# The output projection in fp16 pairs, with Wo and attn scaled

## The chip, the cores and the metric

The kernel runs on one core of one Trainium2 chip. The metric is the device time of one execution in microseconds (us). The time before is 435.67, the median of 3 runs (434.54 to 435.75).

## The reference

One cross-attention layer, with all inputs and outputs in fp32. x is 2 x 2048 x 640, the context 2 x 77 x 1024, with 20 heads of 32. The image part (ip) is empty, since the context has just the 77 text rows.

```
q = split_heads(x @ Wq.T);  k = split_heads(ctx @ Wk.T);  v = split_heads(ctx @ Wv.T)
probs = softmax(q @ k.T / sqrt(32))
out = merge_heads(probs @ v) @ Wo.T + bo + x
```

## The kernel before

Everything is held transposed: channels on the 128 partitions, tokens along the free dimension. The 4096 tokens make NB = 8 tiles of TB = 512 tokens; 640 channels make G = 5 groups of 128 channels, each with HG = 4 heads.

To keep the precision of fp32 at TensorE's fast rates, each large product is made of two parts per operand. An operand a is split into a_hi, a rounded to the narrower kind of number, and a_lo = a - a_hi. `project` (L668) then makes three matmuls per chunk of 128 input channels: w_hi with a_hi, w_lo with a_hi, and w_hi with a_lo. Queries (ps_q) and outputs (ps_o) use pairs of fp32r; probabilities and values use pairs of fp16, where v was divided by the largest value of its channel (v_scale, L515 to L526), which `normalise` (L562) multiplies back in.

The work is a software pipeline, written out by hand per engine. A step (t, g) is one head group g of one token tile t. In step (t, g) the kernel makes the scores and exponentials of (t, g), the max scores of the next group, the query projection of the group after that, the values and the normalisation of the previous group, and one output tile of the previous token tile (`out_tiles`, L63). Every engine runs the same sequence of steps in its own fixed program order (`run`, L118), and semaphores carry the dependencies. Order on TensorE in a steady step (L850 to L889): values of the last group (four column tiles of 32 at once), scores 0 and 1, max scores 0 and 1, output chunks 0 and 1, max scores 2 and 3, scores 2, output chunks 2 and 3, scores 3, transpose of the maxima, output chunk 4, then the whole query projection of 15 matmuls. Steps up to (1, 0) are the fill (L796): the value projections take the place of the outputs. The last token tile's outputs are made at the end, chunk by chunk, in five banks (`last_tiles`, L770).

- ACT: x_hi (L385), k_diag, wq_hi and wo_hi (`w_high`, L400), q_hi (L414), attn_hi (L421), two exponentials per score tile, p_f in fp32 and p_hi in fp16 (L428, L432), and the copy of the transposed maxima (L439). It also issues the loads of the residual x_res and the stores.
- POOL: x_lo (L325), p_lo (L334), attn_lo (L340), wq_lo, wo_lo (L355).
- DVE: the maxima (L548), v_scale, q_lo (L541), the inverse of the denominator and `normalise` (L552 to L566), `finish_out` (L574), which adds bias and residual to ps_o.
- SP: loads of x and the weights, and the DMAs that pack q_hi, q_lo and the maxima into q_packed (`pack_q`, L288; `load_max`, L283).

## Time and profile before

| | |
|---|---|
| median of 3 runs | 435.67 us |
| the profiled execution | 436.16 us, its span 434.4 us |
| mean granted TensorE clock | 0.995 |
| PE busy (matmul) | 426.1 us, 98% of the span, 2538 instructions |
| PE weight load | 313.9 us, 72% |
| POOL | 300.5 us, 69% |
| ACT | 253.9 us, 58% |
| DVE | 232.7 us, 54% |
| share of PE in the chain that ended last | 94% |

The profile is of one execution. Its span runs from the first to the last instruction; the execution's own time also holds what lies around it. PE's busy time counts a matmul from start to modelled end, and matmuls overlap. A row of the order of time that ends in xN merges N instructions. The fp32r matmuls appear as f32 in the rows.

### The profile page before, as it was taken

Reading aid. Unit: us, or ns where it says so; the run is one execution under the profiler, and the core shown is the slowest. Engines: PE = TensorE matmul, PEld = TensorE weight load, DVE = VectorE, ACT = ScalarE, POOL = GpSimd, SP = SyncE. Lnnn points to the kernel's source line nnn. Section 1 sums busy time; section 2 is a strip of 40 time slices with the busy share of each in tenths; the row PEclk is TensorE's granted clock in tenths of the full one; section 3 lists DMA queues with packets and bytes.
Section 4 is the critical chain, followed back from the end, with each engine's and each line's share of the span. In section 5 each row is a group of like instructions: output and inputs, shape, how many; then the busy total and the mean of one; then the engine's idle time right before and its main releaser. Section 6 shows DMA issues by size and latency. Waiting matters only on the chain.

```text
span 434.4 us, 8258 instructions
## 1 busy us (share of the span) xinstructions
PE 426.1 (98%) x2538; PEld 313.9 (72%) x2538; DVE 232.7 (54%) x437; ACT 253.9 (58%) x509; POOL 300.5 (69%) x256
## 2 busy tenths in 40 slices
PE   8999999899999999999999999999999999999996
PEld 6977765677777777777777677777777677777675
DVE  0354766455545555555544555555554455555553
ACT  1737987657465755748464755757564755754510
POOL 8427799989568765959658674959658674955540
PEclk9999999899999999999999999999999999999999
DMA  8997545443455345543355335543355334444203
GB/s 288 359 351 230 203 135 196 146 146 127 145 191 174 122 151 205 205 146 123 135 186 190 123 130 206 204 166 123 125 195 189 124 121 150 157 157 146 75 24 121
DMA packets 39614, 72.68 MB, mean 167 GB/s; under 512 B 5024, under 2 KB 6176, under 8 KB 39584
## 3 DMA queue, kind: packets, MB, share of 16 engines
q1 hardware_dynamic: 28784, 52.62, 34.2%
q10 hardware_dynamic: 10800, 19.67, 14.0%
q8 instruction: 18, 0.29, 0.3%
q14 instruction: 12, 0.10, 0.1%
HBM read 28.81 MB, written 10.49 MB: 90 GB/s over the span
## 4 chain that ended last, share of the span: by engine, by line
PE 94%; POOL 2%; ACT 1%; DVE 1%; issue 1%; DMA 0%; POOLq 0%; ACTq 0%
PE ps_q L673 30%; PE ps_o L673 27%; PE ps_s L731 10%; PE ps_pv L738 7%; PE ps_m L717 5%; PE ps_den L743 4%; PE ps_o L656 2%; POOL p_lo L334 1%; PE ps_m L784 1%; PE ps_s L643 1%; PE ps_m L722 1%; PE ps_q L784 1%; PE ps_q L635 1%; DVE x_f L578 1%; PE ps_o L784 1%
## 5 line engine op out<-in xcount | busy, mean ns | idle before, releaser
L334 POOL TENSOR_TENSOR p_lo<-p_f,p_hi 77x512 f16<-77x512 f32 x160 | 183.2, 1166 | 99.8 <-ACT p_hi L432 97.8
L428 ACT ACTIVATE p_f<-ps_s 77x512 f32<-77x512 f32 x160 | 94.7, 592 | 47.6 <-PE ps_s L731 47.6
L548 DVE TENSOR_REDUCE mx<-ps_m 128x4 f32<-128x308 f32 x160 | 69.3, 475 | 57.7 <-PE ps_m L717 57.4
L432 ACT ACTIVATE p_hi<-ps_s 77x512 f16<-77x512 f32 x160 | 93.5, 584 | 3.0 <-PE ps_den L743 3.0
L541 DVE TENSOR_TENSOR q_lo<-ps_q,q_hi 128x512 fp32r<-128x512 f32 x40 | 27.7, 692 | 101.8 <-ACT q_hi L414 101.8
L673 PE MATMUL ps_q<-x_hi,wq_hi 128*128 128x512 f32 x200 | 79.4, 397 | 0.2 <-POOL wq_lo L348 0.2
L673 PE MATMUL ps_q<-x_lo,wq_hi 128*128 128x512 f32 x200 | 78.3, 391 | 0.0
L673 PE MATMUL ps_q<-x_hi,wq_lo 128*128 128x512 f32 x200 | 78.2, 391 | 0.0
L673 PE MATMUL ps_o<-attn_hi,wo_hi 128*128 128x512 f32 x170 | 70.0, 411 | 0.0
L673 PE MATMUL ps_o<-attn_hi,wo_lo 128*128 128x512 f32 x170 | 67.4, 397 | 0.0
L673 PE MATMUL ps_o<-attn_lo,wo_hi 128*128 128x512 f32 x170 | 67.4, 396 | 0.0
L414 ACT CAST q_hi<-ps_q 128x512 fp32r<-128x512 f32 x40 | 23.4, 584 | 72.3 <-PE ps_q L673 72.0
L731 PE MATMUL ps_s<-q_packed,k_packed 128*77 128x512 f32 x160 | 58.7, 410 | 0.3
L325 POOL TENSOR_TENSOR x_lo<-x_f,x_hi 128x512 fp32r<-128x512 f32 x38 | 48.1, 1300 | 5.9 <-ACT x_hi L385 5.8
L340 POOL TENSOR_TENSOR attn_lo<-attn,attn_hi 128x512 fp32r<-128x512 f32 x38 | 48.5, 1299 | 4.3 <-ACT attn_hi L421 4.3
L673 PEld LDWEIGHTS ps_q<-x_hi,wq_hi 128*128 128x128 f32 x200 | 37.6, 188 | 10.1 <-issue 1.9
L673 PEld LDWEIGHTS ps_q<-x_lo,wq_hi 128*128 128x128 f32 x200 | 37.6, 188 | 8.1
L673 PEld LDWEIGHTS ps_q<-x_hi,wq_lo 128*128 128x128 f32 x200 | 37.6, 188 | 7.7
L673 PEld LDWEIGHTS ps_o<-attn_hi,wo_hi 128*128 128x128 f32 x170 | 32.3, 190 | 7.9
L673 PEld LDWEIGHTS ps_o<-attn_lo,wo_hi 128*128 128x128 f32 x170 | 32.2, 189 | 7.2
L717 PE MATMUL ps_m<-k_diag,q_hi 128*128 128x308 f32 x160 | 37.2, 313 | 0.0
L717 PEld LDWEIGHTS ps_m<-k_diag,q_hi 128*128 128x128 f32 x160 | 30.0, 190 | 9.2 <-issue 0.8
(105 smaller groups left out, 522.1 us busy)
## 6 DMA issues: line engine op xcount, KB each, us to landing
q_packed<-q_hi SPq DMA_DIRECT2D x80, 256.0 KB, 2.5
x_f<-in_x SPq DMA_DIRECT2D x40, 256.0 KB, 3.3
q_packed<-q_lo SPq DMA_DIRECT2D x40, 256.0 KB, 3.2
x_res<-in_x ACTq DMA_DIRECT2D x35, 256.0 KB, 2.7
out<-out_sb ACTq DMA_DIRECT2D x35, 256.0 KB, 2.6
wk_sb<-in_wk SPq DMA_DIRECT2D x8, 320.0 KB, 5.4
wv_sb<-in_wv SPq DMA_DIRECT2D x5, 512.0 KB, 5.9
wq_sb<-in_wq SPq DMA_DIRECT2D x5, 320.0 KB, 5.6
```

Source lines behind the costliest of these rows:

```text
L325: nc.gpsimd.tensor_tensor(x_lo[:, c, :], x_f[:, c, :], x_hi[:, c, :].bitcast(F32), ALU.subtract).then_inc(xlo_pool, 1)
L334: nc.gpsimd.tensor_tensor(p_lo[:, i, :], p_f[:, i, :], p_hi[:, i, :], ALU.subtract).then_inc(plo_done, 1)
L340: nc.gpsimd.tensor_tensor(attn_lo[:, c, :], attn[:, c, :], attn_hi[:, c, :].bitcast(F32), ALU.subtract).then_inc(alo_pool, 1)
L414: nc.scalar.copy(q_hi[:, g % RS, :], ps_q[:, :]).then_inc(qhi_done, 1)
L428: nc.scalar.activation(p_f[:, i, :], ps_s[i % 2][0:L, :], ACT.Exp, scale=SCALE).then_inc(pf_done, 1)
L432: nc.scalar.activation(p_hi[:, i, :], ps_s[i % 2][0:L, :], ACT.Exp, scale=SCALE).then_inc(phi_done, 1)
L541: nc.vector.tensor_tensor(q_lo[:, g % RS, :], ps_q[:, :], q_hi[:, g % RS, :].bitcast(F32), ALU.subtract).then_inc(qlo_done, 1)
L548: nc.vector.tensor_reduce(mx[:, g % RS, :, tt], ps_m[tt % 2][:, 0:HG * L].rearrange("p (h k) -> p h k", k=L), AX_X, ALU.max).then_inc(max_ ...
L673: last = nc.tensor.matmul(ps[:, :], w[:, k, P * c:P * (c + 1)], a[:, c, :], start=(c == 0 and n == 0), stop=(c == G - 1 and n == 2))
L717: nc.tensor.matmul(ps_m[tt % 2][:, 0:HG * L], q_hi[:, g % RS, P * tt:P * (tt + 1)], k_diag[:, g, b, :], start=True, stop=True).then_inc(ms ...
L731: nc.tensor.matmul(ps_s[i % 2][0:L, :], k_packed[:, i, g, L * b:L * (b + 1)], q_packed[:, g % RS, i, :], start=True, stop=True).then_inc(s ...
L738: nc.tensor.matmul(ps_pv[D * i:D * (i + 1), :], v[:, b, P * g + D * i:P * g + D * (i + 1)], p[:, i, :], tile_position=(0, D * i), **flags)
```

## The change

The output projection goes from pairs of fp32r to pairs of fp16. fp16 has a narrow range, so both operands are scaled to the upper part of it, by numbers that the kernel finds itself:

- Wo, per group k of output channels: the largest magnitude in each partition of Wo's group (`wo_largest`, in DVE's steps (0, 1) and (0, 2)) goes into `tops`; a matmul with a matrix of ones (`sum_wo`, in PE's step (0, 3)) sums these over the partitions; the group is multiplied in place by 2^15 over that sum (`wo_scale`).
- attn: the largest v_scale of each partition is summed over partitions in the same way (`sum_v`, in PE's step (0, 4)). `normalise` multiplies by v_rel = v_scale x 2^15 / sum in place of v_scale. The first four groups of token tile 0 come before that number is known: they are normalised without a scale, and `rescale` multiplies them afterwards.
- The product of both scales is taken back in `finish_out` by out_scale in the instruction that added the bias. The bias is added by ACT instead, to the residual (`add_bias`), or to x_f for the last token tile (`add_last_bias`), between the first and the second pair of exponentials of each step.
- Wo's loads stand in SP's steps (-1, 4) and (0, 0), behind pack_q; they stood in steps (0, 0) to (0, 3), before pack_q. wo_hi is made in the same steps as wo_lo; wo_lo's steps are changed as shown. wo_sb no longer shares its place with wo_lo.

The diff, cut to its core:

```diff
+    def wo_top_at(t, g):
+
+        return {(0, 1): ((0,), (1,)), (0, 2): ((2,), (3, 4))}.get((t, g), ((), ())) if isinstance(t, int) else ((), ())
+
+    def wo_scale_at(t, g):
+
+        return {(0, 3): (0, 1), (1, 0): (2, 3), (1, 1): (4,)}.get((t, g), ()) if isinstance(t, int) else ()
...
-        return {(0, 3): (0,), (0, 4): (1, 2), (1, 1): (3, 4)}.get((t, g), ()) if isinstance(t, int) else ()
+        return {(0, 4): (0,), (1, 1): (1, 2, 3), (1, 3): (4,)}.get((t, g), ()) if isinstance(t, int) else ()
...
-        wo_hi = sb("wo_hi", [P, G, C], F32R)
-        with ExitStack() as start_up:
-            wo_sb = sb("wo_sb", [P, G, C], F32, start_up)
-        wo_lo = sb("wo_lo", [P, G, C], F32R)
+        wo_sb = sb("wo_sb", [P, G, C], F32)
+        wo_hi = sb("wo_hi", [P, G, C], F16)
+        wo_lo = sb("wo_lo", [P, G, C], F16)
...
-        attn_hi = sb("attn_hi", [P, G, TB], F32R)
-        attn_lo = sb("attn_lo", [P, G, TB], F32R)
+        attn_hi = sb("attn_hi", [P, G, TB], F16)
+        attn_lo = sb("attn_lo", [P, G, TB], F16)
...
+                if exists(shift(t, g, 2)[0]):
+                    pack_q(*shift(t, g, 2))
                 for c in wo_chunks(t, g):
                     sp.dma_start(wo_sb[:, c, :], wo[:, c, :]).then_inc(wo_in[c], 16)
-                if exists(shift(t, g, 2)[0]):
-                    pack_q(*shift(t, g, 2))
...
+            def add_bias(t, k):
+                act.wait_ge(res_in[k % RS], 16 * slot_uses(t, k))
+                nc.scalar.add(x_res[:, k % RS, :], x_res[:, k % RS, :], bias[:, k:k + 1]).then_inc(res_done, 1)
+
+            def add_last_bias(k):
+                act.wait_ge(xlo_pool, G * NB - len(FIRST_DVE))
+                nc.scalar.add(x_f[:, k, :], x_f[:, k, :], bias[:, k:k + 1]).then_inc(last_biased, 1)
...
                     exponentials(t, g, 0)
+                for tile in out_tiles(t, g):
+                    add_bias(*tile)
+                if is_last(t):
+                    add_last_bias(g)
+                if exists(t):
                     exponentials(t, g, 1)
...
+            def wo_largest(groups):
+                for k in groups:
+                    dve.wait_ge(wo_in[k], 16)
+                    nc.vector.tensor_reduce(tops[:, k:k + 1], wo_sb[:, k, :], AX_X, ALU.max,
+                                            apply_absolute_value=True).then_inc(tops_done, 1)
+
+            def v_largest():
+                dve.wait_ge(vscale_done, 3 * G)
+                nc.vector.tensor_reduce(tops[:, G:G + 1], v_scale[:, :], AX_X, ALU.max).then_inc(tops_done, 1)
+
+            def find_wo_scales():
+
+                dve.wait_ge(wo_summed, 1)
+                nc.vector.tensor_scalar(sums[:, 0:G], ps_wsum, TINY, None, ALU.max).then_inc(scale_done, 1)
+                dve.wait_ge(scale_done, 1)
+                nc.vector.reciprocal(ups[:, 0:G], sums[:, 0:G]).then_inc(scale_done, 1)
+
+            def find_v_scale():
+
+                dve.wait_ge(v_summed, 1)
+                nc.vector.tensor_scalar(sums[:, G:G + 1], ps_vsum, TINY, None, ALU.max).then_inc(scale_done, 1)
+                dve.wait_ge(scale_done, 3)
+                nc.vector.reciprocal(ups[:, G:G + 1], sums[:, G:G + 1]).then_inc(scale_done, 1)
+                nc.vector.tensor_scalar(out_scale[:, :], sums[:, 0:G], sums[:, G:G + 1], 1.0 / (UP * UP),
+                                        ALU.mult, ALU.mult).then_inc(scale_done, 1)
+                dve.wait_ge(scale_done, 4)
+                nc.vector.tensor_scalar(v_rel[:, :], v_scale[:, :], ups[:, G:G + 1], UP,
+                                        ALU.mult, ALU.mult).then_inc(scale_done, 1)
+                dve.wait_ge(scale_done, 6)
+
+            def wo_scale(groups):
+                if groups:
+                    dve.wait_ge(scale_done, 2)
+                for k in groups:
+                    nc.vector.tensor_scalar(wo_sb[:, k, :], wo_sb[:, k, :], ups[:, k:k + 1], UP,
+                                            ALU.mult, ALU.mult).then_inc(wo_scaled, 1)
+
+            def rescale(g):
+
+                dve.wait_ge(norm_done, g + 1)
+                nc.vector.tensor_scalar(attn[:, g, :], attn[:, g, :], v_rel[:, g:g + 1], None,
+                                        ALU.mult).then_inc(rescaled, 1)
...
+                if isinstance(t, int) and t == 0 and g < G - 1:
+                    nc.vector.tensor_tensor(attn[:, g, :], ps_pv[:, :], rden[:, :], ALU.mult).then_inc(norm_done, 1)
+                    return
+                nc.vector.scalar_tensor_tensor(attn[:, g, :], ps_pv[:, :], v_rel[:, g:g + 1], rden[:, :],
...
-                nc.vector.scalar_tensor_tensor(out_sb[:, k % RS, :], out_bank(t, k)[:, :], bias[:, k:k + 1],
-                                               x_res[:, k % RS, :], ALU.add, ALU.add).then_inc(outs_done, 1)
+                nc.vector.scalar_tensor_tensor(out_sb[:, k % RS, :], out_bank(t, k)[:, :], out_scale[:, k:k + 1],
+                                               x_res[:, k % RS, :], ALU.mult, ALU.add).then_inc(outs_done, 1)
...
+                if is_scaling(*shift(t, g, -1)):
+                    rescale(2)
+                    rescale(3)
...
                     q_low(*shift(t, g, 2))
+                if is_scaling(t, g):
+                    rescale(0)
+                    rescale(1)
+                wo_scale(wo_scale_at(t, g))
...
+            def sum_wo(t, g):
+
+                pe.wait_ge(max_done, TT * nth(t, g) + 1)
+                pe.wait_ge(ones_done, 1)
+                pe.wait_ge(tops_done, G)
+                nc.tensor.matmul(ps_wsum, all_ones[:, :], tops[:, 0:G], start=True, stop=True).then_inc(wo_summed, 1)
+
+            def sum_v():
+
+                pe.wait_ge(tops_done, G + 1)
+                pe.wait_ge(vlo_done, G)
+                nc.tensor.matmul(ps_vsum, all_ones[:, :], tops[:, G:G + 1], start=True,
+                                 stop=True).then_inc(v_summed, 1)
```

## Rows read from the trace of the kernel before

**Rows 1.** The page: busy us, share of the span, instructions; then the chain by line.
```profile
PE 426.1 (98%) x2538; PEld 313.9 (72%) x2538; DVE 232.7 (54%) x437; ACT 253.9 (58%) x509; POOL 300.5 (69%) x256
...
PE ps_q L673 30%; PE ps_o L673 27%; PE ps_s L731 10%; PE ps_pv L738 7%; PE ps_m L717 5%; PE ps_den L743 4%; PE ps_o L656 2%; POOL p_lo L334 1%; PE ps_m L784 1%; PE ps_s L643 1%; PE ps_m L722 1%; PE ps_q L784 1%; PE ps_q L635 1%; DVE x_f L578 1%; PE ps_o L784 1%
```
**Rows 2.** Waits of PE: who waited for whom, us in total, times, longest.
```profile
PE ps_pv L738 <- POOL p_lo L334: 1.9, 2, 1.5
```
**Rows 3.** PE in order of time, one steady step: start, duration, what, [idle before].
```profile
211.23 0.39 PE L673 MATMUL ps_o<-attn_hi,wo_hi 128*128 128x512 f32 x1
...
212.39 0.40 PE L673 MATMUL ps_o<-attn_lo,wo_hi 128*128 128x512 f32 x1
...
215.55 0.40 PE L673 MATMUL ps_q<-x_hi,wq_hi 128*128 128x512 f32 x1
...
218.73 0.39 PE L673 MATMUL ps_q<-x_lo,wq_hi 128*128 128x512 f32 x1
219.05 0.40 PE L738 MATMUL ps_pv<-p_hi,v_hi 77*32 77x512 f16 x4
...
219.92 0.39 PE L743 MATMUL ps_den<-p_lo,ones 77*32 77x512 f16 x4
```
**Rows 4.** Stretches: length, then busy PE, PEld, DVE, ACT, POOL, PE clock, DMA, GB/s.
```profile
81.50:84.90 3.40, 3.40 (x11) 2.72 (x10) 0.87 (x2) 2.04 (x4) 3.40 (x4) 0.50 0.57 206
...
170.10:219.20 49.10, 49.10 (x299) 36.01 (x295) 27.10 (x50) 30.12 (x60) 35.25 (x30) 1.00 0.46 161
```
**Rows 5.** PE in order of time: first and last of 45 matmuls at the end.
```profile
420.61 0.39 PE L784 MATMUL ps_q<-attn_hi,wo_hi 128*128 128x512 f32 x1
...
430.58 0.39 PE L784 MATMUL ps_s<-attn_lo,wo_hi 128*128 128x512 f32 x1
```
**Rows 6.** Groups: xcount, busy us, mean ns of one, idle before and what ended it.
```profile
L673 PE MATMUL ps_o<-attn_hi,wo_hi 128*128 128x512 f32 x170 | 70.0, 411 | 0.0
...
L385 ACT CAST x_hi<-x_f 128x512 fp32r<-128x512 f32 x40 | 24.5, 620 | 2.8 <-PE ps_q L673 1.5
...
L521 DVE TENSOR_SCALAR v_scale<-v_scale 128x1 f32<-128x1 f32 x5 | 0.8, 153 | 0.2
```
**Rows 7.** Weight loads in order of time, in the warm-up at the start.
```profile
3.15 0.15 PEld L635 LDWEIGHTS ps_q<-v_hi 77*128 77x128 f16 x1 [0.28 <-issue]
...
4.00 0.15 PEld L635 LDWEIGHTS ps_q<-v_hi 77*128 77x128 f16 x1 [0.28 <-issue]
```
**Rows 8.** ACT, POOL and PE in order of time, step (4, 0) and the next.
```profile
229.08 0.58 ACT L414 CAST q_hi<-ps_q 128x512 fp32r<-128x512 f32 x1 [1.33 <-PE ps_q L673]
...
225.49 2.29 POOL L334 TENSOR_TENSOR p_lo<-p_f,p_hi 77x512 f16<-77x512 f32 x2
...
229.55 0.39 PE L738 MATMUL ps_pv<-p_lo,v_hi 77*32 77x512 f16 x4
```
**Rows 9.** DMA issues: engine, op, xcount, KB each, median us to landing.
```profile
wo_sb<-in_wo SPq DMA_DIRECT2D x5, 320.0 KB, 3.3
```
**Rows 10.** POOL, PE, ACT, DVE in order of time, around steps (1, 0) and (1, 1).
```profile
71.68 3.08 POOL L355 TENSOR_TENSOR wo_lo<-wo_sb,wo_hi 128x640 fp32r<-128x640 f32 x2
...
80.56 0.40 PE L738 MATMUL ps_pv<-p_lo,v_hi 77*32 77x512 f16 x4 [1.47 <-POOL p_lo L334]
...
77.90 1.64 ACT L421 CAST attn_hi<-attn 128x512 fp32r<-128x512 f32 x3
79.44 0.57 ACT L414 CAST q_hi<-ps_q 128x512 fp32r<-128x512 f32 x1
...
77.21 0.75 DVE L566 SCALAR_TENSOR_TENSOR attn<-ps_pv,v_scale,rden 128x512 f32<-128x512 f32 x1
...
82.24 0.87 DVE L548 TENSOR_REDUCE mx<-ps_m 128x4 f32<-128x308 f32 x2 [1.50 <-PE ps_m L717]
```
**Rows 11.** Two lines of DVE: xcount, ns min/median/max, first and last start, forms.
```profile
L571 DVE TENSOR_TENSOR attn_lo<-attn,attn_hi x2: 1774/2228/2682, 412.3 to 414.9; 128x512 fp32r<-128x512 f32 x2
...
L536 DVE TENSOR_TENSOR x_lo<-x_f,x_hi x2: 685/952/1219, 14.9 to 16.1; 128x512 fp32r<-128x512 f32 x2
```

More of the change, by code:

```diff
@@ L37, in xattn_kernel @@
     TINY = 1e-30
+    UP = 2.0 ** 15
     WARM_UP = 8
@@ L212, in xattn_kernel @@
         ps_v, ps_vt = ps_o[:, 0:BL], ps_o[0:L, 512 - B * P:512]
+        ps_wsum, ps_vsum = ps_m[0][:, HG * L:HG * L + G], ps_o[:, 0:1]
         ps_last = [ps_q, ps_m[0], ps_m[1], ps_o, ps_s[0]]
@@ L339, in attn_low @@
                     pool.wait_ge(ahi_done, G * t + c + 1)
-                    nc.gpsimd.tensor_tensor(attn_lo[:, c, :], attn[:, c, :], attn_hi[:, c, :].bitcast(F32),
+                    nc.gpsimd.tensor_tensor(attn_lo[:, c, :], attn[:, c, :], attn_hi[:, c, :],
                                             ALU.subtract).then_inc(alo_pool, 1)
@@ L418, in attn_high @@
                     act.wait_ge(norm_done, G * t + c + 1)
+                    if isinstance(t, int) and t == 0 and c < G - 1:
+                        act.wait_ge(rescaled, c + 1)
                     if exists(t - 1):
@@ L570, in attn_low @@
                 dve.wait_ge(ahi_done, G * t + c + 1)
-                nc.vector.tensor_tensor(attn_lo[:, c, :], attn[:, c, :], attn_hi[:, c, :].bitcast(F32),
+                nc.vector.tensor_tensor(attn_lo[:, c, :], attn[:, c, :], attn_hi[:, c, :],
                                         ALU.subtract).then_inc(alo_dve, 1)
@@ L767, in project_out @@
                     pe.wait_ge(outs_done, nth(t, k))
+                elif chunks[0] == 0:
+                    pe.wait_ge(scale_done, 3)
                 project(out_bank(t, k), wo_hi, wo_lo, attn_hi, attn_lo, k, chunks, ready, o_chunks)
```

47 lines of the change are left out of this document (38 added, 9 removed).

## The prediction

> **What bounds the kernel now.** I read the page's busy times and its chain, then TensorE's waits, then its order of time. PE is busy for 98% of the span, and the largest part of the chain that ended last is PE's query projection [rows 1]. In the whole span PE waits 1.9 us for another engine, in two waits, the longest 1.5 us [rows 2]. So an edit changes the time only if it changes the pace at which PE starts matmuls, or opens a wait. Busy time says nothing of the pace, since a matmul lasts 0.39 us and the next starts before it ends; the reader has to subtract starts. In one steady step the six ps_o matmuls from 211.23 to 212.39 are 1.16 / 5 = 0.232 us apart, the fifteen fp32r matmuls of ps_q from 215.55 to 218.73 are 3.18 / 14 = 0.227 apart, and the five fp16 groups of the values from 219.05 to 219.92 are 0.87 / 4 = 0.2175 apart, though all stream 512 columns [rows 3]. The granted clock is 1.00 there, the 2.4 GHz level [rows 4], at which 512 columns take 0.2133 us. fp16 runs near that floor, fp32r 0.014 to 0.019 above it. At the end, where hardly anything else runs, 45 matmuls start in 9.97 us, 0.2266 apart [rows 5]: that excess comes with fp32r, and up to 0.005 more while other engines work. The change can win only this small excess, many times.
>
> **The PE stream.** No matmul is removed. ps_o has 170 triples [rows 6] and the one tile that is made in ps_q five more: 525 matmuls between other work. last_tiles has 5 x 5 x 3 = 75. The nearest row to a 128x128 fp16 weight load with 512 columns at the higher clock is the values' 0.2175, with loads of 32 columns and three extra starts in each group of four. Below stands the floor, 0.2133; above, nothing changes, 0.232. I take 0.216. The warm-up does load 128 fp16 columns, but its starts, 3.15 to 4.00 over two, are 0.425 apart [rows 7], which is 512 columns at 1.2 GHz: any excess that small is hidden at the lower level. Interleaved: 525 x (0.232 - 0.216) = 8.4 us. The end: 75 x (0.2266 - 0.216) = 0.8 us. Together -9.2 us (the floor would give -10.8, the values' own pace -8.3).
>
> PE loses time where it goes from the whole array to the values' four column tiles: 218.73 to 219.05 is 0.32, some 0.10 over the pace [rows 3]. After the change TensorE alternates between fp16 and fp32r six times a step (into and out of ps_o at the max scores, the scores and the transposed maxima), always on the whole array. Below 0; above 0.10 each, since that boundary is one of number kind as well as of tiles. I take 0, because the tiles are reason enough for it; the other reading is the first rival. The Trainium skill, TensorEngine Tiling (Array Packing), section Key Properties, says that changing the tiling mode drains TensorE, and names no drain for a change of number kind. By that rule the alternations are free and the sum stands.
>
> Two matmuls are added, ones times tops, of 5 and of 1 columns: below 0, above a 512-column one each, 0.46 together. I take +0.3.
>
> **ACT.** Each step with an output tile gains one pass over 128x512 between the first and second pair of exponentials; x_hi, of that shape, takes 0.62 [rows 6]. ACT was busy 30.12 of 49.1 us over five steps [rows 4]. Behind the pass stand the exponentials, copy_max, and in step 0 of a tile the attn_hi casts. That is the tightest step: ACT still idled 1.33 before q_hi at 229.08, and the last p_lo ended at 227.78 for a matmul that started at 229.55, 1.77 of slack [rows 8]. 0.6 fits into both, also with a step 15 x 0.016 = 0.24 shorter. The residual it waits for was ordered one step earlier. Cost 0; without that cover up to 0.6 in each of some 35 steps, 21 us, which the slack excludes. finish_out keeps its form with one add made a multiply: 0. Wo's five casts move later and were hidden: 0.
>
> **SP.** Wo's five loads go into two early steps, behind pack_q instead of before it; one lands in 3.3 us [rows 9]. The packed queries come up to 1 us earlier, the next transposed maxima queue behind Wo's loads. From -1 to +3.3; I take 0, since the maxima are ordered some us after those loads.
>
> **DVE and POOL, once, in the fill.** DVE gains five reductions over Wo, seven tiny instructions (v_scale's take 0.153 each, [rows 6]), a reduction over v_scale, five scalings of Wo and four rescalings of attn. Most stand where DVE waits for PE; 0 for these, up to 1 if the two scale computations hold the maxima. The narrow place is 77 to 86 us. There the values waited 1.47 for p_lo until 80.56, since POOL had two wo_lo, 3.08 us, ahead of that step's p_lo [rows 10]. One of them moves to step (1,1): from -1.5 to 0; I take -0.7, since the exponentials are late next. But behind the normalise that ends at 77.96 come two rescalings, and attn_hi of chunks 2 to 4, which began at 77.90, now waits for them; q_hi (79.44) is behind these on ACT, the max scores wait for q_hi on PE, and the scalings of Wo's chunks 2 and 3 stand before the max reductions that began at 82.24 [rows 10], for which PE waits too. No row has a scaling in SBUF. The nearest is a DVE subtraction of 128x512: 0.685 at its fastest, 1.774 and 2.682 while POOL works beside it [rows 11]; POOL is busy here. Below 0.3 (half the fastest), above 2.7 each. At 0.7 each PE hardly notices; at 2.2 the first two hold q_hi to about 83.5, 2 us late, and the scalings add up to 2. I take +1.2 in all. The low clock after the wait (0.50 for 3.4 us, [rows 4]) costs 1.7; I leave it standing. Net here +0.5, between -3.2 (no wait, no low clock) and +4.
>
> In this the trace agrees in kind with the Trainium skill, SBUF — State Buffer, section Who interferes with whom, on the port pair that VectorE and GpSimd share: one instruction of VectorE or GpSimd holds it whole, and a tensor_scalar between SBUF tiles can need it, so a rescaling would wait out one POOL instruction. By it each costs under 2 us, and the net would be +0.5 to +1.
>
> **Sum** against the profiled execution (436.16, its span 434.4): -9.2 + 0.3 + 0.5 = -8.4, so 427.8. The median of the runs, 435.67, is 0.5 lower: **427.3**. With every term at its low end 436.2 - 10.8 - 3.2 = 422.2, or 421.7 by the median; at its high end 436.2 - 8.3 + 0.5 + 4 = 432.4, or 431.9.
>
> **Rivals.** First, slower: each alternation of fp16 and fp32r drains PE as the tiles' boundary does. Place: six per step in 35 steps, 210 in all. Price: 0.10 each, 21 us, so 427.3 + 21 = 448. It turns the result at 8.4 / 210 = 0.04 us each. For it: every boundary of fp16 and fp32r in the steady trace carries 0.1. Against it: all of these are tile boundaries too. Chance 0.11.
>
> Second, no gain: the 0.014 belongs to loading 128 columns of weights, and the values are fast since they load 32. Then the stream stays, and 435.7 + 0.8 = 436.5. For it: no row separates the two. Against it: the weight load of ps_o lasts less than a start-to-start interval in a pace of 0.227 and lies beside a matmul. Chance 0.08.
>
> Third, the stream wins, but the place at 77 to 86 us costs its +4: 427.3 + 3.5 = 430.8. For it: the two slow subtractions beside POOL; against it, POOL waits in that step for ACT, and leaves DVE room. Chance 0.10. The forecast keeps 0.71.
>
> The range 423.5 to 434 holds the forecast and the third rival and leaves out the others, 0.19. A measurement here can tell 0.3% from no change, 1.3 us. Faster: 0.71 + 0.10 = 0.81; the same: 0.08; slower: 0.11.
>
> **What would show it.** ps_o starts about 0.216 apart, and the last 45 in 9.5 us; five steady steps in about 47.9 and not 49.1, with no wait of PE in them; max scores to ps_o and back without a new gap; each rescaling's duration, and what PE waits for between 77 and 86 us. A pace of 0.227 or more in ps_o, or 0.3 between an fp16 and an fp32r matmul on the whole array, makes the forecast wrong.

## The result: 0.6% slower, and the profile after

The changed kernel takes 437.97 us (median of 20 runs, 435.35 to 444.96), the kernel before 435.69 (20 runs, 434.3 to 436.7): ratio 1.0057, 95% interval 1.0037 to 1.0078. The forecast was 427.3 us. Ratios here and below are of fast runs alone, and so leave out 444.96 and one run of the experiment wo768, 845.39. The profiled execution took 438.97, its span 437.2.

The page after, busy times and chain, against [rows 1]:
```profile
PE 423.4 (97%) x2542; PEld 259.5 (59%) x2542; DVE 247.2 (57%) x458; ACT 275.0 (63%) x549; POOL 296.1 (68%) x257
...
PE ps_q L791 29%; PE ps_o L791 25%; PE ps_s L849 9%; PE ps_pv L856 7%; PE ps_m L835 5%; PE ps_den L861 4%; DMA q_packed<-mxT 3%; PE ps_o L760 1%; DVE attn L611 1%; PE ps_m L904 1%; PE ps_s L747 1%; PE ps_m L840 1%; PE ps_q L739 1%; PE ps_q L904 1%; ACT p_hi L461 1%
```
TensorE's waits after, against [rows 2]: who waited for whom, us in total, times, longest.
```profile
PE ps_m L835 <- ACT q_hi L441: 3.1, 1, 3.1
PE ps_s L849 <- DMA q_packed<-mxT: 1.8, 2, 0.9
...
PE ps_m L835 <- DVE mx L634: 1.1, 1, 1.1
PE ps_s L849 <- ACT p_hi L461: 0.6, 2, 0.3
```
PE's busy time fell by 2.7 us, as an fp16 matmul starts sooner. But VectorE's `attn L611`, one of the new rescalings, is in the chain, and these four kinds of wait are new, 6.6 us together. The 1.9 us for p_lo are gone.

The PE stream after in order of time, against [rows 3]: query matmuls, then output matmuls, then the change from fp16 to fp32r (in the last three lines).
```profile
211.08 0.39 PE L791 MATMUL ps_q<-x_hi,wq_hi 128*128 128x512 f32 x1
...
213.66 0.40 PE L791 MATMUL ps_q<-x_lo,wq_hi 128*128 128x512 f32 x1
...
217.81 0.39 PE L791 MATMUL ps_o<-attn_hi,wo_hi 128*128 128x512 f16 x1
...
218.90 0.38 PE L791 MATMUL ps_o<-attn_lo,wo_hi 128*128 128x512 f16 x1
...
219.89 0.38 PE L791 MATMUL ps_o<-attn_lo,wo_hi 128*128 128x512 f16 x1
219.92 0.58 PE L791 MATMUL ps_q<-x_hi,wq_hi 128*128 128x512 f32 x1
220.34 0.39 PE L791 MATMUL ps_q<-x_hi,wq_lo 128*128 128x512 f32 x1
```
The output matmuls are 1.09 / 5 = 0.218 apart by these rounded starts, 0.216 over all steps. At a change of type the next start is shown after 0.03 and the one behind it after 0.42, together 0.45 for two matmuls, which at their own paces would take 0.216 + 0.234: little is lost. What nobody touched got slower: the query matmuls are (213.66 - 211.08) / 11 = 0.2345 apart, where they were 0.227.

At the end, against [rows 5]: 44 intervals in 9.50 us, 0.216.
```profile
423.58 0.38 PE L904 MATMUL ps_s<-attn_lo,wo_hi 128*128 128x512 f16 x1
...
433.08 0.38 PE L904 MATMUL ps_s<-attn_hi,wo_lo 128*128 128x512 f16 x1
```
VectorE, POOL (GpSimd) and ScalarE after in the narrow place, against [rows 10]: start, duration, line, what. An x2 row holds two instructions.
```profile
72.43 2.22 DVE L594 TENSOR_SCALAR out_scale<-sums 128x5 f32<-128x5 f32 x1
...
75.42 1.78 DVE L611 TENSOR_SCALAR attn<-attn,v_rel 128x512 f32<-128x512 f32 x2
77.12 1.84 DVE L634 TENSOR_REDUCE mx<-ps_m 128x4 f32<-128x308 f32 x4
...
81.32 3.64 DVE L611 TENSOR_SCALAR attn<-attn,v_rel 128x512 f32<-128x512 f32 x2
86.69 0.69 DVE L627 TENSOR_TENSOR q_lo<-ps_q,q_hi 128x512 fp32r<-128x512 f32 x1 [1.74 <-ACT q_hi L441]
87.30 2.42 DVE L605 TENSOR_SCALAR wo_sb<-wo_sb,ups 128x640 f32<-128x640 f32 x2
...
73.22 1.40 POOL L377 TENSOR_TENSOR wo_lo<-wo_sb,wo_hi 128x640 f16<-128x640 f32 x1
...
82.17 2.50 POOL L362 TENSOR_TENSOR attn_lo<-attn,attn_hi 128x512 f16<-128x512 f32 x2
...
85.04 0.62 ACT L450 CAST attn_hi<-attn 128x512 f16<-128x512 f32 x1 [1.79 <-DVE attn L611]
...
86.09 0.57 ACT L441 CAST q_hi<-ps_q 128x512 fp32r<-128x512 f32 x1
```
Five elements a partition take VectorE 2.22 us: `out_scale` ends at 74.65, POOL's `wo_lo` at 74.62. The second pair of rescalings ends at 84.96, 0.29 after POOL's two `attn_lo`. The maxima begin late behind the first pair. Behind the second come ScalarE's copies, behind these q_hi, at 86.09 and not at 79.44, and behind q_hi TensorE's `ps_m`, which waits 3.1 us.

Stretches after, against [rows 4]: 3.4 us at half clock come again, after the wait of 3.1, and 49.1 us of the steady state are as full of PE as before.
```profile
86.70:90.10 3.40, 3.38 (x8) 1.28 (x8) 3.40 (x5) 2.62 (x5) 3.19 (x4) 0.51 0.73 275
170.10:219.20 49.10, 49.10 (x299) 29.68 (x298) 27.53 (x52) 33.04 (x67) 35.05 (x31) 1.00 0.46 162
```
Where the time goes is read best from the first matmul of each group's values, which opens the next step. Below are these starts in order of time; the four right-hand kernels are experiments told of further on (pairs: the fp16 pairs alone; pad: the change with its tensors shifted; Wo: pad without attn's scaling; Wo, ACT: that with Wo's scaling on ScalarE and the last biases spread).
```
values of   before   after   pairs     pad      Wo  Wo,ACT
(0,1)        48.20   49.53   48.10   49.49   48.11   49.05
(0,4)        72.03   73.62   71.95   73.51   71.94   72.89
(1,0)        78.26   81.75   78.19   81.65   78.19   79.12
(1,1)        91.34   96.92   89.04   96.78   91.77   89.58
(1,2)       101.16  107.01   98.72  106.85  101.83   99.86
(7,1)       386.14  388.92  378.65  386.80  381.78  379.80
(7,2)       395.95  398.63  388.29  396.44  391.42  389.43
(7,3)       405.80  408.63  397.74  406.42  401.40  398.89
(7,4)       415.87  419.36  407.40  417.14  412.12  409.00
span         434.4   437.2   425.2   435.0   429.9   426.8
```
From before to after, 5.85 us are lost by (1,2): 1.33 by (0,1), 0.26 more by (0,4), 1.90 in the step to (1,0), which holds out_scale and the first pair of rescalings, and 2.36 from there, with the second pair. The 1.33 don't come in every run: the column Wo has the same loads and maxima of Wo up to there, and 48.11. The 29 steady steps from (1,2) to (7,1) win back only 3.07: each takes 9.721 us in place of 9.827, 0.11 less, where 0.24 was forecast. From (7,1) to (7,4) 0.7 are lost, and the outputs at the end win as much.

### The profile page after: what moved, and what is told of

Read it like the earlier page. It is cut to its first block, busy times and chain, and to the rows that moved or that the text cites. A ratio compares the mean times of both kernels' runs of the same rounds, so it can differ in the third digit from the quotient of the medians.

```text
span 437.2 us, 8356 instructions
## 1 busy us (share of the span) xinstructions
PE 423.4 (97%) x2542; PEld 259.5 (59%) x2542; DVE 247.2 (57%) x458; ACT 275.0 (63%) x549; POOL 296.1 (68%) x257
## 4 chain that ended last, share of the span: by engine, by line
PE 89%; DVE 4%; DMA 3%; ACT 2%; issue 2%; DVEq 0%; ACTq 0%
PE ps_q L791 29%; PE ps_o L791 25%; PE ps_s L849 9%; PE ps_pv L856 7%; PE ps_m L835 5%; PE ps_den L861 4%; DMA q_packed<-mxT 3%; PE ps_o L760 1%; DVE attn L611 1%; PE ps_m L904 1%; PE ps_s L747 1%; PE ps_m L840 1%; PE ps_q L739 1%; PE ps_q L904 1%; ACT p_hi L461 1%
## 5 line engine op out<-in xcount | busy, mean ns | idle before, releaser
L791 PE MATMUL ps_q<-x_hi,wq_hi 128*128 128x512 f32 x200 | 86.7, 433 | 0.5 <-DVE q_lo L627 0.2
L849 PE MATMUL ps_s<-q_packed,k_packed 128*77 128x512 f32 x160 | 65.1, 448 | 2.6 <-DMA q_packed<-mxT 1.8
L791 PE MATMUL ps_o<-attn_hi,wo_hi 128*128 128x512 f16 x170 | 65.6, 386 | 0.0
L791 PE MATMUL ps_o<-attn_lo,wo_hi 128*128 128x512 f16 x170 | 64.9, 382 | 0.0
L791 PE MATMUL ps_o<-attn_hi,wo_lo 128*128 128x512 f16 x170 | 64.9, 382 | 0.0
L835 PE MATMUL ps_m<-k_diag,q_hi 128*128 128x308 f32 x160 | 44.0, 353 | 4.2 <-ACT q_hi L441 3.1
L362 POOL TENSOR_TENSOR attn_lo<-attn,attn_hi 128x512 f16<-128x512 f32 x38 | 44.0, 1180 | 4.8 <-ACT attn_hi L450 4.8
L849 PEld LDWEIGHTS ps_s<-q_packed,k_packed 128*77 128x77 f32 x160 | 20.3, 146 | 24.1 <-issue 14.4
L791 PEld LDWEIGHTS ps_o<-attn_hi,wo_hi 128*128 128x128 f16 x170 | 16.5, 97 | 24.1 <-issue 8.6
```

Source lines behind the costliest of these rows:

```text
L362: nc.gpsimd.tensor_tensor(attn_lo[:, c, :], attn[:, c, :], attn_hi[:, c, :], ALU.subtract).then_inc(alo_pool, 1)
L791: last = nc.tensor.matmul(ps[:, :], w[:, k, P * c:P * (c + 1)], a[:, c, :], start=(c == 0 and n == 0), stop=(c == G - 1 and n == 2))
L835: nc.tensor.matmul(ps_m[tt % 2][:, 0:HG * L], q_hi[:, g % RS, P * tt:P * (tt + 1)], k_diag[:, g, b, :], start=True, stop=True).then_inc(ms ...
L849: nc.tensor.matmul(ps_s[i % 2][0:L, :], k_packed[:, i, g, L * b:L * (b + 1)], q_packed[:, g % RS, i, :], start=True, stop=True).then_inc(s ...
```

## The experiments

Ratios are to the kernel before, on the same chip, with their 95% intervals; 0.001 is 0.44 us. Each trace is of one run. A cut in an edit is marked by ..., and remarks behind # are mine.

**Places of the operands.** The change puts 672 bytes a partition of small tensors ahead of x_hi, x_lo and the packed queries. Three kernels move operands and nothing else:
```diff
         all_ones = sb("all_ones", [P, P], F32)
+        pad = sb("pad", [P, 24], F32)     # place768: 96 bytes; place704: [P, 8], 32 bytes
         k_packed = sb("k_packed", [P, HG, G, BL], F32R)
```
before32 has the pad of 32 bytes ahead of k_packed in the kernel before, behind the weights wo_hi and wo_lo.

> The kernel after, with a pad of 96 bytes a partition behind the six new small tensors, so that they take 768 bytes in place of 672 and x_hi, x_lo, q_hi, q_packed and the rest start at multiples of 128 bytes again, as in the kernel before (in after they start 32 bytes past one). No instruction is changed. Theory A (the places of the operands slow the fp32r matmuls): the 15 query matmuls of a step, 233.8 ns each in after and 227.8 in before, go back to 228; over 35 steps 15 x 0.006 x 35 = 3.1 us, and the maxima with them: 1.0057 - 0.007 = 0.998 to 0.999 of the kernel before, 434.6 to 435.2 us. Rival B (they are slowed by something else in after: the fp16 matmuls before them, other transfers, other traffic of the engines): the pace stays at 233.8 and the ratio at 1.004 to 1.008.

> The same with a pad of 32 bytes: all that stands behind it starts 64 bytes past a multiple of 128, on a multiple of 64. Theory A with a boundary of 64 bytes: query matmuls at 228 ns and 0.998 to 0.999 of the kernel before, as with the pad of 96 bytes. Theory A with a boundary of 128 bytes: 233.8 ns and 1.004 to 1.008. Rival B: no change, 1.004 to 1.008, whatever the pad of 96 bytes shows would have to be the same here.

> The kernel before with one unused tensor of 32 bytes a partition ahead of k_packed, so that all behind it stands 32 bytes further; no instruction is changed and nothing is in fp16 pairs. Theory A: both the query and the output projection read moved activations, so 30 matmuls of a step go from 228 to 234 ns: 30 x 0.006 x 40 = 7.2 us, 441 to 443.5 us, ratio 1.012 to 1.018. Rival B: no change, 435.7 us, ratio within 0.003 of 1.

Measured: place768 1.0023 (1.0000 to 1.0046), place704 1.0058 (1.0030 to 1.0085), before32 1.0103 (1.0079 to 1.0127). Query matmuls in order of time, place768, then before32:
```profile
219.42 0.39 PE L792 MATMUL ps_q<-x_hi,wq_lo 128*128 128x512 f32 x1
...
222.40 0.39 PE L792 MATMUL ps_q<-x_lo,wq_hi 128*128 128x512 f32 x1
```
```profile
215.92 0.40 PE L674 MATMUL ps_q<-x_hi,wq_hi 128*128 128x512 f32 x1
...
219.18 0.39 PE L674 MATMUL ps_q<-x_lo,wq_hi 128*128 128x512 f32 x1
```
2.98 / 13 = 0.229 with x_hi on a multiple of 128 bytes, 3.26 / 14 = 0.233 at 32 past it, with no fp16 weights at all, and 0.233 at 64 past it (place704, whose ratio is as expected, too). By these paces theory A holds, with 128 bytes as the boundary. The steady step of the change goes from 9.721 to 9.653 with the pad of 96 bytes, and to 9.706 with that of 32. By the ratio place768 won about half of what was expected, and its interval overlaps those of place704 and of the change: that it saves time at all rests on the traces. before32 lost less than was expected (4.5 us, not 7.2), since its output matmuls between other work slow by 0.002, not 0.006. At its end, where hardly anything else runs, they slow by 0.007, against [rows 5]:
```profile
423.40 0.39 PE L785 MATMUL ps_q<-attn_hi,wo_hi 128*128 128x512 f32 x1
...
433.67 0.39 PE L785 MATMUL ps_s<-attn_lo,wo_hi 128*128 128x512 f32 x1
```
That is 10.27 / 44 = 0.233 where it was 0.2266. The weights of these matmuls had not moved, only the moving operands, attn's highs and lows. The output matmuls of the change, in fp16 at 0.216, have the same pace with and without the shift: of these two, only fp32r pays.

**The early Wo loads.**
```diff
-        return {-1: (0, 1), 0: (2, 3, 4)}.get(nth(t, g), ()) if isinstance(t, int) else ()
+        return {-1: (0,), 0: (1, 2), 1: (3, 4)}.get(nth(t, g), ()) if isinstance(t, int) else ()
```


> The kernel after with the five Wo loads spread 1, 2, 2 over the steps (-1,4), (0,0) and (0,1) in place of 2, 3 over the first two. The transposed maxima of group 1 landed at 48.87 us in after (issued at 43.82, behind three Wo loads of 640 KB in all) and at 46.70 in before. Theory C (these loads hold up the maxima): they land about 1 us earlier, the wait of 0.92 us of the scores at 48.9 us is down to under 0.3, and the kernel is 0.6 to 1.2 us faster than after: 436.8 to 437.4, ratio 1.003 to 1.004. Rival: the wait is another's or the gain is given back at the next waits of the fill: 1.0045 to 1.007.

Measured: 1.0164 (1.0129 to 1.0198), 4.7 us slower than the change by the ratios. VectorE's waits between 38 and 60 us:
```profile
DVE tops L574 <- DMA wo_sb<-in_wo: 5.0, 2, 4.4
```
The maxima of Wo stayed where they were, so VectorE, in order, stood 4.4 us for its own load. That priced a mistake of the experiment, not the theory, which f_loads below tries again.

**VectorE's scalings: their form, and their engine.** Both on place768. forms768 writes each rescaling as
```diff
-                nc.vector.tensor_scalar(attn[:, g, :], attn[:, g, :], v_rel[:, g:g + 1], None,
-                                        ALU.mult).then_inc(rescaled, 1)
+                nc.vector.scalar_tensor_tensor(
+                    attn[:, g, :].rearrange("p (a b) -> p a b", b=P),
+                    attn[:, g, :].rearrange("p (a b) -> p a b", b=P), v_rel[:, g:g + 1],
+                    all_ones[:, :].unsqueeze(1).to_broadcast([P, TB // P, P]), ALU.mult, ALU.mult).then_inc(rescaled, 1)
```
and Wo's scalings, out_scale and v_rel likewise with two tensors. act768 takes the same scalings out of VectorE's stream and puts them into ScalarE's, for attn
```diff
+                        nc.scalar.mul(attn[:, c, :], attn[:, c, :], v_rel[:, c:c + 1]).then_inc(rescaled, 1)
```
ahead of the wait and the copy in attn_high, and for Wo in the same way in wo_high.

> The kernel after with the pad of 96 bytes, and with another form of VectorE instruction for the scalings that the change added on SBUF operands: the four rescalings of attn, the five of Wo, out_scale and v_rel were tensor_scalar (one tensor read) and are now scalar_tensor_tensor or tensor_tensor (two tensors read; the second is a tensor of ones or the scale itself). The same products on the same engine at the same place of its stream, and the 2^15 is folded into the sums. In after the nine tensor_scalar of 128x512 and 128x640 took 1.2 to 3.6 us each and the one of 128x5 2.22, while POOL's subtractions ran; normalise, a two-tensor form of 128x512, took 0.69 beside the same subtractions. Theory A (a one-tensor SBUF form of VectorE waits for GpSimd's running operation): each rescaling takes 0.7 us, out_scale 0.2; the values of group (0,4) and after, 3.4 us late against before at 81.65 us and 5.7 at 106.85, come about 1.5 and 3 us earlier: 2.0 to 3.5 us under the kernel with the pad alone, ratio 0.994 to 0.998. Rival B (they are long because of what they wait for, or in any form): the rescalings stay over 1.5 us and the ratio at 1.0023.

> The kernel after with the pad of 96 bytes, and with the rescalings of attn and of Wo, v_rel and out_scale moved from VectorE to ScalarE, which does each directly ahead of the copy to fp16 that it does anyway. Theory A (the loss of the fill is VectorE's scalings, each 1.2 to 3.6 us long beside GpSimd): VectorE's maxima and q_lo come early again, ScalarE carries nine passes more of 0.7 us, four of them in the step that starts at 81.65 us, so 1 to 3 us are won and up to 1 lost on ScalarE: ratio 0.995 to 1.001. Rival B (what bounds the narrow place is ScalarE's chain through q_hi, which these passes now lengthen by 2.8 us): the values of step (1,1) come no earlier than 96.8 us and the ratio is 1.002 to 1.009.

Measured: forms768 1.0057 (1.0031 to 1.0083), not faster than place768 (the intervals overlap; in the profiled runs it is 3.1 us later at (1,2)); act768 0.9979 (0.9965 to 0.9993), 1.9 us faster than place768, as its theory A had it. Groups of VectorE between 70 and 95 us, forms768:
```profile
L615 DVE SCALAR_TENSOR_TENSOR attn<-attn,v_rel,all_ones 128x512 f32<-128x512 f32 x4 | 6.4, 1650 | 0.0
...
L596 DVE TENSOR_TENSOR out_scale<-sums 128x5 f32<-128x5 f32 x1 | 2.3, 2260 | 0.0
```
My idea that only the one-tensor form waits was wrong: the two-tensor form waits as well, 1.65 each. (The 3.6 us in the expectation is a row of two instructions: singly the rescalings of the change took 0.48, 1.39, 1.22 and 2.49.) normalise and q_lo, of the same size, take 0.75 and 0.69 in the same stretch: they read one tensor from PSUM and one from SBUF, the scalings read only SBUF. The Trainium skill, SBUF — State Buffer, section Who interferes with whom, has both halves: a tensor_scalar between SBUF tiles can take the pair of ports that VectorE shares with GpSimd, and two inputs in SBUF contend with a GpSimd instruction that reads SBUF. The traces agree with both, by the 1.39 to 2.49 of the one form beside POOL and the 1.65 of the other. They also show more than one instruction waited for: the last rescaling of the change, 2.49 us from 82.46, began while POOL's `attn_lo` of 82.17 to 83.56 ran and ended only after the next one, at 84.95.

**The last biases.**
```diff
-                if is_last(t):
-                    add_last_bias(g)
+                if is_last(t) and g == 0:
+                    add_last_bias(0)
...
+                if is_last(t) and g in (1, 2):      # behind exponential 3
+                    add_last_bias(2 * g - 1)
+                    add_last_bias(2 * g)
```


> The kernel after with the pad of 96 bytes, and with the bias of the last five tiles added at the ends of the steps (7,1) and (7,2), two each, and one in (7,0), in place of one in each of (7,0) to (7,4); (7,3), which has two bias passes of its own, and (7,4) lose one. In after ScalarE's passes there held up the exponentials: waits of 0.31 and 0.26 us of the scores, and 0.6 more ahead of the last tiles; the stretch from the values of (7,3) to the values of the last step took 10.72 us in place of 10.07. Theory: 0.3 to 0.8 us faster than the kernel with the pad alone, ratio 1.0005 to 1.0017, and the stretch is at 10.1 to 10.4. Rival (the stretch is longer by a wait on VectorE or on the alternation): no change, 1.0023 and 10.7.

Measured: 0.9983 (0.9958 to 1.0008). The steps (7,3) and (7,4) take 9.45 and 10.12 us, where place768 has 9.98 and 10.72: 1.1 us. The ratio says 1.7 us, more than was expected, but its interval overlaps that of place768, and the rest lies ahead of the edit, in the fill of the profiled run, so I put 1.1 down to it.

**Price of a change of type.** alt768 is place768, altbefore the kernel before, each with
```diff
-                if tiles:
-                    project_out(*tiles[0], (0, 1))
-                if exists(max_t):
-                    max_scores(max_t, max_g, 2, batch(max_t))
...
+                for c in range(4):
+                    if tiles:
+                        project_out(*tiles[0], (c,))
+                    if exists(max_t) and c < 2:
+                        max_scores(max_t, max_g, 2 + c, batch(max_t))
+                    if exists(t) and c == 2:
+                        scores(t, g, 2, batch(t))
```

> The kernel after with the pad of 96 bytes; in each steady step the fp16 output matmuls are cut finer, by groups of three: three, one fp32r matmul of maxima, three, maxima, three, scores 2, three, where it was six, two of maxima, scores 2, six. That makes 10 changes of type a step in place of 6. Step now 9.65 us. By the 0.05 us a step that six changes seem to cost (7.834 us of the stretch of output, maxima, scores and query matmuls less 0.24 of pace would be 7.594, measured 7.643), four more cost 0.03: 9.68. By the rival of the prediction, 0.10 each, 10.05. Nothing but the order is changed; the same order in the kernel before is the control, to be run after this.

> The control: the kernel before, all fp32r in these matmuls, with the same finer order of output, maxima and score matmuls (three, maxima, three, maxima, three, scores, three). There is no change of type in it. Step now 9.82. If the step of the fp16 kernel with this order (9.733 against 9.65) is longer by the four more changes of type (0.02 each), this one stays at 9.82 within 0.02. If it is by the order itself, 9.90.

Measured, over the 29 steady steps: alt768 9.757 against 9.653, +0.104; altbefore 9.869 against 9.827, +0.042. alt768 is above the 9.68 expected, altbefore between its 9.82 and 9.90: the order itself costs 0.04, and four more changes of type 0.062, 0.015 each, by one profiled run of either kernel. Six of them would be 0.09 a step. The steady step gives less. With the pad it is 0.17 shorter than before; the output matmuls of the kernel before start 0.2305 apart in the mean of all steady steps, not 0.232 as in the step of [rows 3], so the pace wins 15 x 0.0145 = 0.22, and 0.05 are left, 0.008 for each of the six.

**The fp16 pairs alone.** This is the kernel before with Wo's and attn's pairs in fp16, without any scale, with bias and loads as before; wo_sb gets a place of its own, as in the change.
```diff
-        wo_hi = sb("wo_hi", [P, G, C], F32R)
+        wo_hi = sb("wo_hi", [P, G, C], F16)       # wo_lo, attn_hi, attn_lo likewise
```


> The kernel before with one part of the change alone: Wo's and attn's highs and lows are fp16 in place of fp32r. It leaves out all scaling of the change (the maxima and sums of Wo, the rescalings, out_scale) and the moved bias, so the lows of Wo and attn lose low bits. Every tensor behind the Wo ones stands where it stands in the kernel before, on a multiple of 128 bytes. Theory: the steady step is at 9.65 us as in the kernel after with the pad of 96 bytes (9.82 before), which gives 35 x 0.17 = 6.0 us, the end 0.7 more, and the fill loses nothing, since what it lost were the scalings beside GpSimd and the early Wo loads: 428.5 to 430, ratio 0.984 to 0.988. Rival: the fill loses its time by the alternation or by the clock as well, 432 to 434, ratio 0.992 to 0.996.

Measured: 427.01 us, 0.9816 (0.9800 to 0.9833), 8.0 us faster and better than expected; five runs within 0.23 us. The steady step is at 9.653, as with the pad. The granted clock in the stretch of [rows 4]:
```profile
81.50:84.90 3.40, 3.40 (x19) 1.75 (x18) 2.61 (x7) 2.71 (x6) 3.40 (x4) 1.00 0.54 197
```
It holds 2.4 GHz here, after a wait for p_lo of 1.0 us in place of 1.5, and is 2.4 us ahead by (1,2). This was not in the expectation. The kernel before itself does both: of its 90 runs beside the experiments, 51 have a mean clock of 0.998 or more and a median of 434.58 us, 38 have 0.995 or 0.996 and 435.95. So a stretch at half clock costs it 1.4 us, and against its runs without one the pairs win 7.6. None of the 20 runs of the change is above 0.996.

**Repairs together.** best2 is act768 with the spread biases; best3 adds later Wo loads, and the maxima with them.

> The kernel after with three repairs: the pad of 96 bytes, the scalings on ScalarE, and the last biases spread over (7,0) to (7,2). Alone the second gave 0.9979 against 1.0023 with the pad alone (2.0 us), the third 0.9983. If they add up: 1.0023 - 0.0044 - 0.001 to 0.004 = 0.994 to 0.997, 432.6 to 434.0. Rival: they share what they gain, since the spread can only bear on the end of the program (0.6 us there) and the rest of its figure was the spread of runs: 0.9965 to 0.998.

> best2 with the Wo loads spread 1, 2, 2 over (-1,4), (0,0), (0,1), as in the kernel that came out slower for it (there VectorE, in order, waited 4.4 us for the Wo load that its maxima need), and now with the maxima of Wo moved behind the loads: groups 0 | 1 | 2 | 3, 4 at the steps (0,1) to (0,3). Theory C (the early loads cost 1.2 us by holding up the transposed maxima on the way in): no wait of VectorE on Wo, 0.5 to 1.3 us faster than best2, ratio 0.0012 to 0.003 under it. Rival: the two maxima in (0,3), 1.6 us ahead of the sum over the partitions, hold up TensorE there, and it is not faster than best2 (0 to 0.003 above it).

Measured: best2 0.9957 (0.9942 to 0.9972), as expected, best3 0.9941 (0.9920 to 0.9962). best3 has its values of (0,1) at 48.17, not 49.11 as best2 (wo768 has 48.11 there with the loads unchanged, so this can be chance), but its profiled span is 1.1 us longer (432.3 against 431.2), with 6.8 us at half clock in the narrow place where best2 has 3.4. The intervals overlap, so its gain is not settled.

**Each part on the pairs alone.** f_rdve and f_ract multiply the four attn chunks by 1.0 on VectorE or on ScalarE, f_loads has the change's Wo loads, f_bias its bias.
```diff
+                nc.vector.tensor_scalar(attn[:, g, :], attn[:, g, :], 1.0, None, ALU.mult).then_inc(rescaled, 1)  # f_rdve
+                nc.scalar.mul(attn[:, c, :], attn[:, c, :], 1.0).then_inc(rescaled, 1)  # f_ract, ahead of its copy
+                for c in {-1: (0, 1), 0: (2, 3, 4)}.get(nth(t, g), ()) if isinstance(t, int) else ():  # f_loads, behind pack_q
+                nc.scalar.add(x_res[:, k % RS, :], x_res[:, k % RS, :], bias[:, k:k + 1]).then_inc(res_done, 1)  # f_bias
```


> The kernel with the fp16 pairs alone (no scales, bias on VectorE, Wo loads at their old places: 427.0 us, 0.9816) and four in-place multiplications of attn by 1.0 on VectorE (tensor_scalar, 128x512), at the places of the change's rescalings and waited for by ScalarE's copies to fp16. Theory A (they wait for GpSimd's running subtraction, and later ones for two): 0.5 us where GpSimd is idle, 1.2 to 2.5 beside it, q_hi of step (1,0) late, a wait of 2 to 3 us of TensorE and then a stretch at the low clock: 2.5 to 5 us, ratio 0.987 to 0.993. Rival B (they are short and hidden here, and only together with the scale computations and loads do they matter): under 1 us, 0.981 to 0.984.

> The same with the four multiplications on ScalarE, each directly ahead of its copy to fp16. Theory A: ScalarE has no turn to wait for, each takes 0.7 us; 1 to 2.5 us, ratio 0.984 to 0.9875, and in any case less than with VectorE. Rival B (any 2.8 us more ahead of q_hi in step (1,0) costs the same, whoever does it): the same ratio as with VectorE within 0.001.

> The kernel with the fp16 pairs alone, and its five Wo loads at the change's places: two in (-1,4), three in (0,0), behind the queries' packing. Nothing else. Theory C (the early loads delay the maxima and the packed queries on the same queues): the values of (0,1), at 48.10 us there and at 49.53 in after, come 0.8 to 1.3 us later; 0.8 to 1.5 us in all, ratio 0.9834 to 0.985. Rival (that delay was VectorE's maxima of Wo, 0.8 us each ahead of the maxima of the scores): 0 to 0.3 us, 0.981 to 0.9825.

> The kernel with the fp16 pairs alone, and the bias as in the change: ScalarE adds it to the residual ahead of exponential 1 of each step, and to the last five tiles in (7,0) to (7,4). Nothing else. Theory: nothing in the steady steps (9.65 us), and 0.5 to 1.7 us at the end, where (7,3) has three passes; ratio 0.983 to 0.9855. Rival (ScalarE's slack hides it there too): 0.981 to 0.9825.

Measured: f_rdve 0.9900 (0.9867 to 0.9933), f_ract 0.9898 (0.9869 to 0.9926), f_loads 0.9831 (0.9802 to 0.9859), f_bias 0.9850 (0.9819 to 0.9880), so 3.7, 3.6, 0.7 and 1.5 us over the pairs alone (each of these differences is uncertain by some 1.5 us, and the last two intervals overlap that of the pairs). VectorE in f_rdve, and what TensorE waited for:
```profile
71.87 4.60 DVE L573 TENSOR_SCALAR attn<-attn 128x512 f32<-128x512 f32 x2
76.39 0.85 DVE L550 TENSOR_REDUCE mx<-ps_m 128x4 f32<-128x308 f32 x2
...
80.80 0.75 DVE L573 TENSOR_SCALAR attn<-attn 128x512 f32<-128x512 f32 x2
```
```profile
PE ps_m L729 <- DVE mx L550: 3.1, 1, 3.1
```
The first pair takes 4.60 us (2.20 and 2.48) beside POOL's two `wo_lo` and two `p_lo`, the second 0.75 (0.42 each) with POOL idle: the same instruction, six times as long, and it holds the maxima. In f_ract each takes 0.61, but two of them and three copies stand between the last exponential and q_hi, two more before:
```profile
79.09 0.61 ACT L420 ACTIVATE attn<-attn 128x512 f32<-128x512 f32 x1
...
81.96 0.58 ACT L414 CAST q_hi<-ps_q 128x512 fp32r<-128x512 f32 x1
```
and the half clock follows, here two of the stretches of f_ract, columns as in [rows 4]:
```profile
82.00:84.00 2.00, 1.57 (x5) 0.82 (x5) 1.43 (x3) 2.00 (x6) 2.00 (x3) 0.50 0.56 176
84.00:86.00 2.00, 2.00 (x6) 0.95 (x5) 0.12 (x1) 0.48 (x1) 2.00 (x3) 0.50 0.92 333
```
Rival B of f_ract held, the same ratio within 0.001, but the two profiled runs lose in different ways. f_rdve adds the wait of 3.1 us and has 3.4 us at half clock. In f_ract TensorE waits at most 1.1 us at a time, for p_hi, p_lo and q_hi, and the half clock lasts 6.8 us, in which output matmuls start 0.43 apart and not 0.216: it costs 3.4. That the ratios are equal may therefore be chance. The loss is shown for either engine, but not that work ahead of q_hi has one price. As expected, f_bias has its 1.6 us in the steps (7,3) and (7,4), 9.99 and 10.72 where the pairs alone have 9.45 and 9.66; its steady step is unchanged. f_loads lies between theory and rival, its profile shows 0.2, and its 0.7 is not clear of noise.

**The Wo part and the attn part, in the whole change.** wo768 is place768 without attn's scaling: the rescalings, v_rel, the sum over v and the second factor of out_scale are left out. wobest moves Wo's scalings to ScalarE as well, and spreads the last biases.
```diff
-                nc.vector.scalar_tensor_tensor(attn[:, g, :], ps_pv[:, :], v_rel[:, g:g + 1], rden[:, :],
+                nc.vector.scalar_tensor_tensor(attn[:, g, :], ps_pv[:, :], v_scale[:, g:g + 1], rden[:, :],
```


> The kernel after with the pad of 96 bytes, and without the scaling of attn: normalise multiplies by v_scale as before the change, and the sum of v's maxima, v_rel, the four rescalings and the second factor of out_scale are left out; out_scale is the sum of Wo's maxima alone. Wo is still loaded early, reduced, summed and scaled on VectorE, and the bias is still on ScalarE. If the attn part costs here what the rescalings cost alone (3.7 us), plus the out_scale that took 2.2 us of VectorE: 4 to 6 us under the kernel with the pad alone, ratio 0.988 to 0.993. If most of the 5 us that are left are Wo's: no more than 3.7 us under it, ratio 0.994 to 0.997.

> The same with Wo's five scalings moved to ScalarE, ahead of its copies, and the last biases spread over (7,0) to (7,2), which won 1.1 us of the 1.6 at the end in two kernels. If VectorE's scalings of Wo (2.4 us at the start of (1,1)) are on the path: 1.5 to 2.5 us under the first, ratio 0.984 to 0.989. If they are hidden: 1.1 us, 0.0025 under it.

Measured: wo768 0.9955 (0.9939 to 0.9971), wobest 428.8 us, 0.9860 (0.9835 to 0.9886). The attn part costs 0.0068, 3.0 us. That is the other branch of the expectation: most of what is left is Wo's. (The two profiled spans are 5.1 apart, but that of wo768, its fastest run, kept the full clock throughout.) Wo's scalings in wo768: xcount, ns min/median/max; then TensorE's longest wait.
```profile
L587 DVE TENSOR_SCALAR wo_sb<-wo_sb,ups x5: 542/1435/2724, 64.8 to 93.1; 128x640 f32<-128x640 f32 x5
```
```profile
PE ps_m L791 <- DVE mx L610: 2.6, 1, 2.6
```
The 2.72 us ran over two of POOL's `attn_lo`, and the maxima came behind it. With them on ScalarE it is 4.1 us less in all, more than the 1.5 to 2.5 expected. 1.1 of it is the spread, seen in (7,3) and (7,4), which leaves 3.0 for moving the scalings of Wo. They are not wholly hidden there: wobest is 1.1 us behind the pairs alone at (1,2). wobest beats the kernel before by 1.4% and keeps Wo's scales; the pairs alone, without any scale, beat it by 1.8%.

## Why the prediction was wrong

- **The PE stream, -9.2.** The pace of 0.216 was right, in both places. The sum was too large: 0.232 was read from one step, and the mean of all steady steps is 0.2305, so 525 x 0.0145 = 7.6 and not 8.4. That the profiled span of the pairs alone is 9.2 below before's is luck: 2.4 of it is the fill, where the clock stayed up, and the steps and the end gave 6.8.
- **Alternation, 0.** Mis-sized: 0.015 each by alt768 and altbefore, 0.008 by the steady step, some 2 to 3 us over 210. The first rival's 0.10 is excluded, and its break-even of 0.04 was not reached.
- **The query matmuls.** No term of the sum and no rival had them: the change shifts fp32r operands off a multiple of 128 bytes. 0.07 a step and 2.2 us of span, 1.5 by the ratios.
- **ACT, 0.** Right in the steady steps; wrong at the end, where I looked at none: step (7,3) has two output tiles and a last bias. 1.5 us.
- **SP, 0.** 0.7 alone, within its bounds and not clear of noise.
- **The waits before.** The prediction has TensorE waiting 1.9 us for other engines in the whole span. The same view has 0.2 more for wq_lo, and in the fill
```profile
PE ps_q L635 <- DVE v_hi L588: 1.5, 1, 1.5
```
Both are there after the change as well, so no term changes.
- **DVE and POOL in the fill, +0.5, between -3.2 and +4.** This is the step that failed. From before to after the kernel is 5.85 us later at (1,2), above even the upper bound. The term looked at 77 to 86 us, and only 2.36 came behind (1,0); 3.49 were lost ahead of it, where the scale computations and the first rescalings stood at 0, or up to 1. Against the pairs alone it is 8.3 at (1,2). Of these, 3.0 to 3.7 go with the rescalings of attn, 3.0 with the scalings of Wo and 0.7 with the loads; the rest was not taken apart. I had the mechanism and bounded one rescaling by 0.3 and 2.7, and 0.48 to 2.49 came. The two rescalings ahead of q_hi took 3.7 us, less than the 4.4 of my slow case, and yet q_hi came at 86.09 and not at 83.5, since that step began 3.5 late. What made it late was left out: out_scale stood among the tiny instructions of 0.153 and took 2.22, and I saw only the maxima at 82 us, not those at 77, behind the first two rescalings. The scalings of Wo were given up to 2 us in all ahead of the maxima; their part was 3.0. And I had a wait cost one instruction of POOL, where it was two at the longest rescaling.
- **The low clock, left standing.** It is not a fixed cost. The pairs alone are free of it in all five runs, the kernel before in more than half of its runs, the change in none of 20; f_rdve, f_ract and best2 have it in their profiled runs. So part of what the waits of the fill cost is this clock, 1.4 us for one stretch by the runs of the kernel before, and how much of the 8.3 it is was not measured apart.

The parts come out near the whole, in us: pairs alone -8.0, places +1.5, bias +1.5, loads +0.7, attn's scaling +3.0 to 3.7, Wo's +3.0 make +1.7 to +2.4; measured is +2.5 by the ratio, whose interval is 0.9 to each side. Each part is uncertain by 1 us or more itself, so this is no proof that none is missing. The sum also takes the parts as independent, which act768 and f_ract show they are not quite: on ScalarE attn's and Wo's scalings together win 1.9 us, attn's alone nothing.

## What to carry to other kernels

Where one engine is full for the whole steady state, price a change's one-time work as carefully as its repeated gain: here some 20 instructions in the fill cost 6 to 7 us, and 600 faster matmuls won 8. Before VectorE gets an instruction that reads only SBUF, look what GpSimd does at that time, and count two of GpSimd's instructions, not one: 2.49 us came here for an instruction that took 0.42 with GpSimd idle. And look where the operands of unchanged matmuls come to lie when tensors are added ahead of them.
